# Two second norms folded into the stages of the first norms (latent attention and Mamba block)

## The chip, the cores and the metric

The kernel runs on one core of a Trainium2 chip. The metric is the device time of one execution in microseconds; the time before is the median of three runs.

## The reference, cut to what matters

Six blocks in a row, each of them added to its input and normalised. The second block begins with a layer norm of the first's already normalised output, the fourth with an RMS norm of the third's.

```python
x = _layernorm(x + _L0_attn_ref(x, ...), axis=-1)
x = _layernorm(x + _L0_xattn_ref(ctx_1024, x, ...), axis=-1)   # begins: ln = layernorm(latents=x, ln_l_g, ln_l_b)
x = _layernorm(x + _L0_ffn_ref(x, ...), axis=-1)
x = _layernorm(x + _L1_attn_ref(x, ...), axis=-1)              # begins: xn = x * rsqrt(mean(x**2) + 1e-6) * norm_scale
x = _layernorm(x + _L1_xattn_ref(x, ctx_1024, ...), axis=-1)
x = _layernorm(x + _L1_ffn_ref(x, ...), axis=-1)
```

x has 32 batches of 56 rows of 128 features, 1792 rows in all, float32. The layer norm has an epsilon of 1e-5. For a row with variance v the first norm's output has mean 0 and variance v / (v + 1e-5), so both norms in a row can be had from v alone: the layer norm of the layer norm divides by the root of (1 + 1e-5) v + 1e-10, the RMS norm of it by the root of (1 + 1e-6) v + 1e-11.

## The kernel before, in words

The rows are held as 16 tiles of 112 rows (`x_tm`), in 4 chunks of 4 tiles. The program is a sequence of blocks; in each, every engine has a written-out queue, and the queues meet by semaphores. Between blocks all engines wait for each other. After the larger stages (`lent_semaphores`, L107) two more barriers and a clearing of semaphores follow.

First place. `stage_scan` runs the first block's scan and leaves its gated result in `gT`, transposed. Then `stage_norm` "l0p" runs: TensorE adds x and the output projection in PSUM (L295, L766), VectorE takes the statistics of each row from there (bn_stats L312, bn_aggr L316), ScalarE the root (L354), VectorE the reciprocal and the normalised rows (L328, L334), written to `x_tm`. The loop on VectorE takes the statistics of chunk c and then normalises chunk c - 1. Barriers follow. `stage_latents` then calls `stage_norm` "bln", which takes statistics of `x_tm` again, writes normalised rows to `keep`, transposes them on TensorE (L301) and evicts them with gain and shift on ScalarE (L366) to `lT`. Beside it SP issues ten small loads and four context loads of 750 KB (L833 to L843), and POOL two memsets. The first eviction waits for the ten small loads. The block after it ("bw") opens with TensorE's products of `lT` (L890).

Second place. `stage_weighed` "f0r" is the tail of the third block (two of eight experts per row): TensorE projects each expert's hidden rows (L1656) into four PSUM banks, half a tile's experts to a bank; VectorE weighs and adds them into `z` (L1577), in a written-out interleaved order, takes statistics (L1592, L1596), reciprocal (L1602) and offset (L1604); ScalarE writes the normalised rows from `z` to `x_tm` (L1560). SP loads the Mamba block's weights beside it. Barriers follow. `stage_mamba` then calls `stage_norm` "min" (an RMS norm: two small products more per chunk, L321 and L323; eviction L364 with the gain to `xnT`), and its next block opens with TensorE's products of `xnT` (L1915).

Of the kernel before, what the change touches and what calls it, by code (L numbers as in the profile page):

```python
# [16 lines left out]
ALU = mybir.AluOpType  # L17
# [25 lines left out]
LN_EPS = 1e-5  # L43
DT_TOP = 0.11
# [127 lines left out]
class MambaWeights:  # L172
# [12 lines left out]
    bout: object  # L185
    loaded: object
# [6 lines left out]
def mamba_weights(core, ctx):  # L193

    H2 = INNER // P
    sb, _ = ctx.enter_context(scope(core, "mw"))
    core.mamba = MambaWeights(
        col=sb("col", [P, H2, 12]), alog=sb("alog", [P, H2, DS]), scale=sb("scale", [D, 1]), win=sb("win", [D, 2 * INNER]),
        wdt_in=sb("wdt_in", [P, H2, MAMBA_R]), wdt_out=sb("wdt_out", [MAMBA_R, INNER]), dtb=sb("dtb", [MAMBA_R, 1]),
        wbc=sb("wbc", [P, H2, P]), bcb=sb("bcb", [P, 1]), wout=sb("wout", [P, H2, D]), bout=sb("bout", [T2, D]),  # L200
        loaded=core.sem("mw_loaded"))
# [59 lines left out]
def stage_norm(core, name, project=None, doubled=False, rms=False, gain=None, shift=None,  # L261
               residual=True, outT=None, beside=None, ready=None):
# [7 lines left out]
    squared, roots = core.shared("n_squared"), core.shared("n_roots")  # L270
    with scope(core, name) as (sb, psum):
        y = psum("y", [P, NC, 512]) if project else None
        xt = psum("xt", [P, NC, 512]) if outT else None
        keep = core.x_tm if residual else sb("keep", [T2, NT, D])
        raw = sb("raw", [T2, NT, 6])
        mv = sb("mv", [T2, NT, 2])
        rstd = sb("rstd", [T2, NT])
        std = sb("std", [T2, NT])
# [7 lines left out]
        with nc.Block() as block:  # L286
# [19 lines left out]
            def _(ve):  # L306
# [18 lines left out]
                def normalise(c):  # L325
                    tiles = slice(c * TPC, (c + 1) * TPC)
                    ve.wait_ge(roots.sem, roots(c + 1))
                    ve.reciprocal(rstd[:, tiles], std[:, tiles]).then_inc(scales.sem, 1)  # L328
                    ve.wait_ge(scales.sem, scales(c + 1))
                    for n in range(c * TPC, (c + 1) * TPC):  # L330
                        if rms:
                            last = ve.tensor_scalar(keep[:, n, :], value(n), rstd[:, n:n + 1], None, ALU.mult)
                        else:
                            last = ve.tensor_scalar(keep[:, n, :], value(n), mv[:, n, 0:1], rstd[:, n:n + 1], ALU.subtract, ALU.mult)  # L334
                    last.then_inc(normed.sem, 1)

                for c in range(NC + 1):
# [6 lines left out]
            def _(act):  # L344
# [3 lines left out]
                for c in range(NC + 2):  # L348
                    if c < NC:
                        if rms:  # L350
                            act.wait_ge(squared.sem, squared(2 * c + 2))
                        else:
                            act.wait_ge(moments.sem, moments(c + 1))
                        act.activation(std[:, c * TPC:(c + 1) * TPC], mv[:, c * TPC:(c + 1) * TPC, 1], ACT.Sqrt,  # L354
                                       bias=eps[0:T2, :]).then_inc(roots.sem, 1)
                    if c >= 2 and outT:
# [24 lines left out]
        roots.base += NC  # L381
        normed.base += NC
# [24 lines left out]
def stage_scan(core):  # L407
# [4 lines left out]
    with scope(core, "l0s") as (sb, psum):  # L412
        gT = sb("gT", [P, 2, T])
        wout = sb("wout", [P, 2, D])

        with scope(core, "l0r") as (sb2, psum2):
            u = sb2("u", [P, RC, TC, 2, W])
            yT = sb2("yT", [P, 2, NCH, TC * B])
            gate = sb2("gate", [P, 2, NCH, TC * B])
            xs = sb2("xs", [P, 2, NCH, TC * B])  # L420
            xr = sb2("xr", [P, NCH, D])
            xnT = sb2("xnT", [D, NCH, TC * B])
            win = sb2("win", [D, 2 * INNER])
            lnw = sb2("lnw", [D, 2])
            raw = sb2("raw", [P, NCH, 6])
            mv = sb2("mv", [P, NCH, 2])
            rstd = sb2("rstd", [P, NCH])
            shift = sb2("shift", [P, NCH])
            eb = sb2("eb", [P, 2, RB // CPG, CPG, DS])
            cexp = sb2("cexp", [P, NG, RB])  # L430
            bcol = sb2("bcol", [P, 2, DS])
            spread = sb2("spread", [P, RB])
            c_gp = sb2("c_gp", [NG, 2, P])
            cA = sb2("cA", [P, 2, NG])
            mine = sb2("mine", [P, CPG])
            a_col = sb2("a_col", [P, 1])
            NPU = 6
            pu = psum2("pu", [P, NPU, 512])
            py = psum2("py", [P, 512])
            pg = psum2("pg", [P, 512])  # L440
            names = ("const built mine turned got spread eb cexp step u_made filled filled_ve y_made y_taken y_gated x_made x_kept "
                     "stats moments lnv rstd shift normed xturned xT").split()
            s = {n: core.sem(f"l0r_{n}") for n in names}
            x_first, x_rest, loads_x, loads_w, loads_p, loads_late = (core.sem(f"l0r_load_{n}") for n in
                                                                    ("first", "rest", "x", "w", "p", "late"))

            half_way = NCH // 2
            WAVES = 4
            FILLS = WAVES * 4
            SHARED = FILLS // 2  # L450

            def scanned(t):

                return 2 + 4 * t

            def wave(w):

                return w // 2, 2 * (w % 2)

            def filling(n):  # L460

                return (s["filled_ve"], n // 2 + 1) if n < FILLS and n % 2 else (s["filled"], n // 2 + 1 if n < FILLS else n - SHARED + 1)

            PAIRS = NCH // 2
            REST = slice(1, NCH - 1)
            def load_x(eng, tiles, sem):
                for k in range(TC):
                    src = d["x"].rearrange("b (j t) d -> t b j d", t=TC)[k]
                    eng.dma_start(xr[k * B:(k + 1) * B, tiles, :], src[:, tiles, :]).then_inc(sem, 16)

            kept = [("x", p) for p in range(RC + 1)]
            for c in range(PAIRS):
                if RC + 1 + c < PAIRS:
                    kept.append(("x", RC + 1 + c))
                kept.append(("gate", c))

            def kept_at(what, p):

                return kept.index((what, p)) + 1

            with nc.Block() as block:
                @block.sync
                def _(sp):
                    sp.dma_start(bcol[:, :, :], d["L0_attn_B_mat"].rearrange("(h p) s -> p h s", p=P)).then_inc(loads_p, 16)
                    load_x(sp, pair_of_chunks(0), x_first)
                    sp.dma_start(c_gp[:, 0, :], d["L0_attn_C_mat"].rearrange("(g i) s -> g (i s)", i=CPG)).then_inc(loads_x, 16)
                    sp.dma_start(c_gp[:, 1, :], d["L0_attn_A_log"].rearrange("(g i) s -> g (i s)", i=CPG)).then_inc(loads_x, 16)
                    sp.wait_ge(x_first, 16 * TC)
                    sp.dma_start(wout[:, :, :], d["L0_attn_out_proj_wT"].rearrange("(h p) d -> p h d", p=P)).then_inc(loads_late, 16)
                    sp.dma_start(core.x_tm[:, :, :], d["x"].rearrange("b t d -> (b t) d")  # L490
                                 .rearrange("(n p) d -> p n d", p=T2)).then_inc(loads_late, 16)
                    sp.wait_ge(loads_late, 32)

                @block.gpsimd
                def _(pool):
# [281 lines left out]
LP = 64  # L777

def stage_attention(core):  # L780

# [1914 lines left out]
```

## Time and profile before

| | us |
|---|---|
| median of three runs | 1248.31 (1247.03 to 1248.79) |
| profiled execution, its own time | 1245.21 |
| its span, first to last instruction | 1243.5 |
| VectorE ends the scan | 244.61 |
| first norm's rows written | 260.08 |
| block after the second norm opens on TensorE | 274.87 |
| expert stage's rows written | 793.45 |
| block after the RMS norm opens on TensorE | 807.04 |

Times in the profile count from the span's start. PE is TensorE's matmul queue and PEld its weight loads, DVE is VectorE, ACT ScalarE, POOL GpSimd, SP the queue that issues loads.
### The profile page before, as it was taken

To read this page: it belongs to the slowest core of one execution; us is meant where nothing else is said; L and a number is where in the kernel's file an instruction comes from. 1 tells how busy PE (TensorE), PEld (TensorE's weight loads), DVE (VectorE), ACT (ScalarE), POOL (GpSimd) and SP (SyncE) were. 2 spreads that over 40 slices of the span, in tenths; PEclk is the share of its full clock that TensorE was granted. 3 is DMA by queue.
4 is the path that set the end of the run, shared out by engine and by line. 5 is a ranking of instruction groups with operands and counts; after the bars stand their busy time and mean duration, and the time that the engine had idled before them with its cause. 6 is when DMAs were issued, how large, how long until landed. Compare 5 with 4: busy or idle time off the path is not lost. (4 is left out here: it accounts for less than half of the span.)

```text
span 1243.5 us, 22989 instructions
## 1 busy us (share of the span) xinstructions
PE 1020.0 (82%) x8317; PEld 742.0 (60%) x8317; DVE 1007.7 (81%) x2073; ACT 714.9 (57%) x1508; POOL 592.1 (48%) x899
## 2 busy tenths in 40 slices
PE   5889996557599999999999698391788888768696
PEld 3555653234599999999998566340333333536555
DVE  5989999665698889889886538778999999577575
ACT  3677673025466666666664263275677777247453
POOL 4200000002798888888884131011799999225360
PEclk9899998768799999999999989795799999879989
DMA  3000000011301211112100010001000000000001
GB/s 74 1 1 2 2 1 1 1 53 60 132 32 71 76 72 67 66 73 76 71 6 2 1 24 1 1 1 42 25 0 1 1 1 1 1 2 3 2 1 30
DMA packets 18770, 33.41 MB, mean 27 GB/s; under 512 B 5201, under 2 KB 13889, under 8 KB 18657
## 3 DMA queue, kind: packets, MB, share of 16 engines
q1 hardware_dynamic: 16768, 30.89, 7.3%
q10 hardware_dynamic: 1888, 1.05, 0.4%
q8 instruction: 66, 1.08, 0.4%
q14 instruction: 48, 0.39, 0.1%
HBM read 31.02 MB, written 0.92 MB: 26 GB/s over the span
## 5 line engine op out<-in xcount | busy, mean ns | idle before, releaser
L2209 POOL TENSOR_TENSOR m_h_in<-m_dtu,m_bs 128x448 f32<-128x448 f32 x128 | 144.3, 1146 | 70.3 <-DVE m_dtu L2253 53.4
L753 DVE SCALAR_TENSOR_TENSOR l0r_u<-l0r_u,l0r_a_col 128x1024 f32<-128x1024 f32 x110 | 135.9, 1276 | 6.0 <-ACT l0r_u L663 6.0
L2276 DVE TENSOR_TENSOR_SCAN m_hs<-msp_da,m_h_in 128x448 f32<-128x448 f32 x128 | 136.0, 1078 | 2.4 <-ACT msp_da L2236 1.7
L1134 POOL TENSOR_TENSOR bl_sc<-bl_sc,bl_topall 125x1456 f32<-125x1456 f32 x32 | 105.3, 3289 | 59.6 <-ACT bl_topall L1296 59.6
L663 ACT ACTIVATE l0r_u<-l0r_pu 128x512 f32<-128x512 f32 x216 | 108.4, 644 | 32.3 <-PE l0r_pu L565 32.2
L2172 PE MATMUL msp_py<-m_hc,ident 128*128 128x448 f32 x256 | 118.1, 546 | 0.0
L565 PE MATMUL l0r_pu<-l0r_xs,l0r_eb 32*128 32x256 f32 x896 | 106.5, 460 | 6.9 <-ACT l0r_u L663 4.6
L846 POOL MEMSET bq_lT<- 128x256 f32 x1 | 0.3, 311 | 222.1 <-POOLq L107 222.1
L1371 PE MATMUL bl_pS<-b_qw,bl_xcT 128*125 128x112 f32 x768 | 104.0, 278 | 0.0
L565 PEld LDWEIGHTS l0r_pu<-l0r_xs,l0r_eb 32*128 32x128 f32 x896 | 73.0, 210 | 39.5 <-ACT l0r_u L663 29.0
L2227 ACT ACTIVATE m_bs<-msp_pb 128x448 f32<-128x448 f32 x128 | 69.2, 541 | 44.9 <-PE msp_pb L2156 43.4
L1303 ACT ACTIVATE bl_sq<-bl_pX 125x512 f32<-125x512 f32 x96 | 57.2, 597 | 63.2 <-PE bl_pX L1360 34.5
L1371 PEld LDWEIGHTS bl_pS<-b_qw,bl_xcT 128*125 128x125 f32 x768 | 91.5, 189 | 0.0
L1360 PE MATMUL bl_pX<-b_mk,bl_xcT 128*125 128x128 f32 x768 | 91.4, 277 | 0.0
L1360 PEld LDWEIGHTS bl_pX<-b_mk,bl_xcT 128*125 128x125 f32 x768 | 88.2, 191 | 0.2 <-ACT bl_xcT L1241 0.2
L1211 DVE TENSOR_REDUCE bl_top<-bl_sc 125x112 f32<-125x1456 f32 x32 | 86.3, 2696 | 1.5 <-DVE bl_sc L1191 0.5
L2236 ACT ACTIVATE msp_da<-m_dt,mw_alog 128x440 f32<-128x440 f32 x128 | 80.2, 627 | 5.5 <-DVE m_hs L2276 5.5
L1191 DVE TENSOR_TENSOR bl_sc<-bl_pS,bl_inv 125x448 f32<-125x448 f32 x96 | 59.1, 620 | 26.9 <-PE bl_pS L1371 26.9
L1225 DVE TENSOR_REDUCE bl_ss<-bl_sq 125x8 f32<-125x512 f32 x96 | 62.7, 680 | 14.3 <-ACT bl_sq L1303 10.4
L2164 PE MATMUL msp_pc<-m_bc,selector 128*128 128x448 bf16 x128 | 47.6, 372 | 31.9 <-DVE m_hc L2262 31.9
L2164 PEld LDWEIGHTS msp_pc<-m_bc,selector 128*128 128x128 bf16 x128 | 12.5, 98 | 102.6 <-DVE m_hc L2262 94.6
L758 DVE TENSOR_SCALAR l0r_u<-l0r_u 128x1024 f32<-128x1024 f32 x112 | 72.0, 683 | 0.0
(396 smaller groups left out, 2527.6 us busy)
## 6 DMA issues: line engine op xcount, KB each, us to landing
b_xc<-in_ctx SPq DMA_DIRECT2D x16, 750.0 KB
bl_more<-in_ctx SPq DMA_DIRECT2D x16, 750.0 KB
x_tm<-in_x SPq DMA_DIRECT2D x1, 896.0 KB, 6.2
cw_cT<-in_ctx_headT SPq DMA_DIRECT2D x1, 896.0 KB
out_dram<-x_tm SPq DMA_DIRECT2D x4, 224.0 KB, 2.5
l0r_xr<-in_x ACTq DMA_DIRECT2D x4, 192.0 KB, 5.5
w_up<-in_L_ffn_w SPq DMA_DIRECT2D x1, 512.0 KB, 4.0
w_down<-in_L_ffn_w SPq DMA_DIRECT2D x1, 512.0 KB, 5.2
```

The costliest lines, as they stand in the source:

```text
L565: last = pe.matmul(out, eb[rows, half, j0 + j, :, :], x, start=True, stop=True)
L663: act.activation(u[:, c % RC, :, :, at:at + 2 * B].rearrange("p t r x -> p (t r) x"), pu[:, n % NPU, :].rearrange("p (a x) -> p a x", x=2 ...
L753: ve.scalar_tensor_tensor(state(c, i, r), prev, a_col[:, :], state(c, i, r), ALU.mult, ALU.add).then_inc(s["step"], 1)
L758: ve.tensor_scalar(state(c, i, r), state(c, i, r), 10.0, -10.0, ALU.min, ALU.max).then_inc(s["step"], 1)
L1134: pool.tensor_tensor(sc[0:KP, n % 3, :, :], sc[0:KP, n % 3, :, :], over(topall[0:KP, n % 2, :].unsqueeze(1), [KP, KT + 1, QR]), ALU.subtra ...
L1211: ve.tensor_reduce(top[0:KP, n % 2, :], sc[0:KP, n % 3, :, :].rearrange("p k q -> p q k"), AX, ALU.max).then_inc(s["top"], 1)
L1360: last = pe.matmul(pX[0:KP, u, r * D:(r + 1) * D], xcT[:, n % 2, at], mk[:, :], start=True, stop=True)
L1371: last = pe.matmul(pS[0:KP, u, r * QR:(r + 1) * QR], xcT[:, n % 2, t * KP:(t + 1) * KP], qw[:, n, :], start=False, stop=(r == KS - 1))
L2172: pe.matmul(py[:, g % 2, 0:CH], core.ident[:, :], hc[:, n % NU, :], start=(st == 0), stop=(st == DS - 1)).then_inc(s["summed"], 1)
L2209: pool.tensor_tensor(h_in[:, n % NU, :], dtu[:, half, cols], bs[:, n % NU, :], ALU.mult).then_inc(s["db"], 1)
L2236: act.activation(da[:, n % 2, 0:CH].rearrange("p (b t) -> p b t", t=L)[:, :, 1:L], dt[:, half, cols].rearrange("p (b t) -> p b t", t=L)[:, ...
L2276: ve.tensor_tensor_scan(hs[:, n % NU, :], da[:, n % 2, 0:CH], h_in[:, n % NU, :], 0.0, ALU.mult, ALU.add).then_inc(s["scan"], 1)
```

## The change

First place: "l0p" and "bln" become one call of `stage_norm`, made by `stage_latents` after the scan's barriers. It takes the row statistics once, computes two roots per chunk, writes the second norm's rows with VectorE to `keep`, and the first norm's rows with ScalarE from PSUM to `x_tm`, in ScalarE's queue ahead of the evictions. ScalarE reads a PSUM bank only after VectorE has done with it. SP's loads and POOL's memsets of "bln" now run beside it. `gT` is now two tensors, the first of them `core.xT`, which is free then; the expert weights' buffers are laid out ahead of the scan.

Second place: the "min" call is gone. In the expert stage VectorE computes both reciprocals and writes the RMS norm's rows to `keep` after each chunk's scale; TensorE transposes them behind its last projection into the banks (`ph`) that the hidden products used; ScalarE evicts them with the gain to `mamba.xnT`.

```diff
 def stage_norm(core, name, project=None, doubled=False, rms=False, gain=None, shift=None,
-               residual=True, outT=None, beside=None, ready=None):
+               residual=True, outT=None, beside=None, ready=None, second=False):
...
-        keep = core.x_tm if residual else sb("keep", [T2, NT, D])
+        keep = core.x_tm if residual and not second else sb("keep", [T2, NT, D])
+        R2 = 2 if second else 1
...
-                    ve.reciprocal(rstd[:, tiles], std[:, tiles]).then_inc(scales.sem, 1)
+                    ve.reciprocal(rstd[:, :, tiles], std[:, :, tiles]).then_inc(scales.sem, 1)
                     ve.wait_ge(scales.sem, scales(c + 1))
+                    if second:
+                        ve.scalar_tensor_tensor(offset[:, tiles], mv[:, tiles, 0], -1.0, rstd[:, 0, tiles], ALU.mult,
+                                                ALU.mult).then_inc(offsets.sem, 1)
...
+                        if second:
+                            if c == 0:
+                                act.wait_ge(offsets.sem, offsets(1))
+                            act.activation(std[:, 1, c * TPC:(c + 1) * TPC], mv[:, c * TPC:(c + 1) * TPC, 1], ACT.Sqrt,
+                                           bias=next_eps[:, :], scale=1.0 + LN_EPS)
...
+                    if second and 1 <= c < NC + 1:
+                        act.wait_ge(offsets.sem, offsets(c + 1))
+                        act.wait_ge(normed.sem, normed(c))
+                        for n in range((c - 1) * TPC, c * TPC):
+                            act.activation(core.x_tm[:, n, :], value(n), ACT.Identity, bias=offset[:, n:n + 1],
+                                           scale=rstd[:, 0, n:n + 1])
                     if c >= 2 and outT:
...
-        stage_norm(core, "l0p", project=project)
+    return project
...
-        stage_norm(core, "bln", residual=False, gain=lng[:, 2:3], shift=lng[:, 3:4],
+        stage_norm(core, "l0p", project=gated_projection, second=True, gain=lng[:, 2:3], shift=lng[:, 3:4],
...
+                opened(pe)
+                for c in range(NC):
+                    pe.wait_ge(s["rows"], c + 1)
+                    for r in range(TPC):
+                        last = pe.transpose(ph[:, c, r * T2:(r + 1) * T2], keep[:, c * TPC + r, :], core.ident[0:T2, 0:T2])
+                    last.then_inc(s["turned"], 1)
...
-                for c in range(NC + 1):
+                act.wait_ge(s["next_eps"], 1)
+                act.wait_ge(core.mamba.loaded, MAMBA_LOADED)
+                for c in range(NC + 2):
                     if c < NC:
                         tiles = slice(c * TPC, (c + 1) * TPC)
                         act.wait_ge(s["moments"], c + 1)
-                        act.activation(std[:, tiles], mv[:, tiles, 1], ACT.Sqrt, bias=core.eps_ln[0:T2, :]).then_inc(s["roots"], 1)
-                    if c:
+                        act.activation(std[:, 0, tiles], mv[:, tiles, 1], ACT.Sqrt, bias=core.eps_ln[0:T2, :])
+                        act.activation(std[:, 1, tiles], mv[:, tiles, 1], ACT.Sqrt, bias=next_eps[:, :],
+                                       scale=1.0 + RMS_EPS).then_inc(s["roots"], 1)
+                    if 1 <= c < NC + 1:
                         act.wait_ge(s["scales"], 2 * c)
...
+                    if c >= 2:
+                        act.wait_ge(s["turned"], c - 1)
+                        act.activation(inputs[:, (c - 2) * CH:(c - 1) * CH], ph[:, c - 2, 0:CH], ACT.Copy, scale=core.mamba.scale[:, 0:1])
...
+                def next_rows(c):
+
+                    ve.wait_ge(s["scales"], 2 * c + 1)
+                    for n in range(c * TPC, (c + 1) * TPC):
+                        last = ve.tensor_scalar(keep[:, n, :], z[:, n, :], mv[:, n, 0:1], rstd[:, 1, n:n + 1], ALU.subtract, ALU.mult)
+                    last.then_inc(s["rows"], 1)
+
                 for c in range(NC + 1):
                     if c < NC:
                         statistics(c)
                     if c:
                         scale_and_offset(c - 1)
+                        next_rows(c - 1)
...
-            stage_norm(core, "min", rms=True, residual=False, gain=scale[:, 0:1], outT=by_batch(xnT),
-                       ready=(core.mamba.loaded, MAMBA_LOADED))
...
-        with lent_semaphores(core):
-            stage_scan(core)
         expert_weights(core)
-        with lent_semaphores(core):
-            stage_attention(core)
+        with ExitStack() as gated_scope:
+            with lent_semaphores(core):
+                gated_projection = stage_scan(core, gated_scope)
+            with lent_semaphores(core):
+                stage_attention(core, gated_projection)
```

## Rows read from the trace of the kernel before

**Rows 1.** The page, busy time by engine
```profile
PE 1020.0 (82%) x8317; PEld 742.0 (60%) x8317; DVE 1007.7 (81%) x2073; ACT 714.9 (57%) x1508; POOL 592.1 (48%) x899
```

**Rows 2.** Timeline around the first place: start us, us, engine, line
```profile
243.51 1.10 DVE L718 TENSOR_TENSOR l0s_gT<-l0r_py,l0r_gate 128x256 f32<-128x256 f32 x2 [7.20 <-PE l0r_py L585]
...
244.94 0.44 PE L295 MATMUL l0p_y<-x_tm,ident 112*112 112x128 f32 x2 [1.50 <-PEq L481]
...
253.15 0.88 DVE L312 BATCH_NORM_STATS2 l0p_raw<-l0p_y 112x6 f32<-112x128 f32 x4
...
255.10 0.60 PE L766 MATMUL l0p_y<-l0s_wout,l0s_gT 128*112 128x128 f32 x4
255.83 0.88 DVE L312 BATCH_NORM_STATS2 l0p_raw<-l0p_y 112x6 f32<-112x128 f32 x4
...
258.71 1.37 DVE L334 TENSOR_SCALAR x_tm<-l0p_y,l0p_mv,l0p_rstd 112x128 f32<-112x128 f32 x4
...
261.75 0.87 DVE L312 BATCH_NORM_STATS2 bln_raw<-x_tm 112x6 f32<-112x128 f32 x4 [1.68 <-PEq L107]
...
264.30 1.11 DVE L334 TENSOR_SCALAR bln_keep<-x_tm,bln_mv,bln_rstd 112x128 f32<-112x128 f32 x4
...
265.47 1.01 PE L301 MATMUL bln_xt<-ident,bln_keep 112*128 112x112 f32 x4 [9.77 <-DVE bln_keep L334]
...
270.47 0.72 ACT L366 ACTIVATE bq_lT<-bln_xt,bq_lng 128x448 f32<-128x448 f32 x1 [3.53 <-DMA bq_mask<-in_mask_BxS_bk]
...
271.28 1.33 ACT L366 ACTIVATE bq_lT<-bln_xt,bq_lng 128x448 f32<-128x448 f32 x2
...
274.87 4.77 PE L890 MATMUL bw_ps<-bq_w,bq_lT 128*128 128x384 f32 x8 [1.06 <-PEq L286]
...
287.35 0.91 PE L890 MATMUL bw_ps<-bq_w,bq_lT 128*128 128x384 f32 x2 [2.33 <-ACT b_vl L962]
```

**Rows 3.** Timeline around the second place
```profile
770.60 0.15 DVE L1602 RECIPROCAL f0r_rstd<-f0r_std 112x4 f32<-112x4 f32 x1
...
770.86 0.34 DVE L1577 SCALAR_TENSOR_TENSOR f0r_z<-f0r_pj,f0r_used,x_tm 112x128 f32<-112x128 f32 x1
...
783.04 3.19 PE L1656 MATMUL f0r_pj<-w_down,f_hidden 128*112 128x128 f32 x24 [1.65 <-DVE f0r_z L1577]
...
789.89 0.14 DVE L1602 RECIPROCAL f0r_rstd<-f0r_std 112x4 f32<-112x4 f32 x1
...
790.27 3.18 ACT L1560 ACTIVATE x_tm<-f0r_z,f0r_offset,f0r_rstd 112x128 f32<-112x128 f32 x8
...
794.58 0.87 DVE L312 BATCH_NORM_STATS2 min_raw<-x_tm 112x6 f32<-112x128 f32 x4 [3.86 <-PEq L107]
...
806.11 0.63 ACT L364 ACTIVATE mi_xnT<-min_xt,mw_scale 128x448 f32<-128x448 f32 x1 [0.37 <-PE min_xt L301]
...
807.04 8.36 PE L1915 MATMUL mip_ps<-mi_xnT,mw_win 128*128 128x448 f32 x16 [0.97 <-PEq L286]
```

**Rows 4.** Windows: PE, PEld, DVE, ACT, POOL busy; PEclk, DMA share, GB/s
```profile
244.90:255.70 10.80, 10.76 (x96) 10.59 (x96) 6.36 (x34) 2.38 (x5) 0.00 (x0) 1.00 0.00 1
255.70:261.00 5.30, 0.00 (x1) 0.00 (x0) 4.27 (x19) 0.30 (x1) 0.00 (x0) 0.75 0.00 0
274.87:278.87 4.00, 4.00 (x7) 2.19 (x8) 0.74 (x8) 1.10 (x4) 0.00 (x0) 0.51 0.33 137
289.00:290.00 1.00, 1.00 (x7) 1.00 (x6) 0.00 (x0) 0.12 (x2) 1.00 (x1) 0.53 0.32 135
770.00:786.00 16.00, 12.32 (x101) 11.11 (x100) 15.77 (x70) 3.82 (x10) 0.00 (x0) 1.00 0.01 2
786.00:794.00 8.00, 0.23 (x3) 0.03 (x1) 4.37 (x21) 3.44 (x9) 0.00 (x0) 0.80 0.00 0
```

**Rows 5.** One line of ScalarE: an affine copy from PSUM, min/median/max ns
```profile
L639 ACT ACTIVATE l0r_xnT<-l0r_pg,l0r_lnw x7: 558/564/637, 10.2 to 92.1; 128x256 f32<-128x256 f32 x7
```

**Rows 6.** Timeline of SP's queue in the expert stage
```profile
725.83 0.47 SPq L223 DMA_DIRECT2D mw_bcb<-in_L_attn_c_proj_b  x1
```

More of the change, by code:

```diff
@@ L43 @@
 LN_EPS = 1e-5
+RMS_EPS = 1e-6
 DT_TOP = 0.11
@@ L185 @@
     bout: object
+    xnT: object
     loaded: object
@@ L269, in stage_norm @@
         core.shared(s) for s in ("n_proj", "n_stats", "n_moments", "n_scales", "n_normed", "n_turned"))
-    squared, roots = core.shared("n_squared"), core.shared("n_roots")
+    squared, roots, offsets = (core.shared(s) for s in ("n_squared", "n_roots", "n_offsets"))
     with scope(core, name) as (sb, psum):
@@ L381, in stage_norm @@
         roots.base += NC
+        offsets.base += NC + 1 if second else 0
         normed.base += NC
@@ L764, in project @@
-        def project(pe, n, out):
-            for h in range(2):
-                last = pe.matmul(out, gT[:, h, n * T2:(n + 1) * T2], wout[:, h, :], start=False, stop=(h == 1))
-            return last
-        stage_norm(core, "l0p", project=project)
+                                if j == 0 and n >= NPU:
+                                    pe.wait_ge(*filling(n - NPU))
+                                rows = slice(gl * RB, (gl + 1) * RB)
+                                out = pu[:, n % NPU, :].rearrange("p (t r j b) -> p j r t b", t=TC, r=2, j=2)[:, j]
@@ new lines, in _ @@
+                pe.wait_ge(s["built"], 1)
+                turn(0)
+                pe.wait_ge(loads_w, 32)
+                project("x", 0)
+                pe.wait_ge(loads_x, 32)
+                for k in range(2):
+                    pe.transpose(pu[:, NPU - 1, k * NG:(k + 1) * NG], c_gp[:, k, :], core.ident[0:NG, 0:NG]).then_inc(s["turned"], 1)
+                pe.wait_ge(s["eb"], 1)
+                pe.wait_ge(s["got"], 2)
+                for c in range(RC):
+                    inputs(c)
+                    turn(c + 1)
+                    project("x", c + 1)
@@ L772, with project @@
+    def project(pe, n, out):
+        for h in range(2):
+            last = pe.matmul(out, gT[h][:, n * T2:(n + 1) * T2], wout[:, h, :], start=False, stop=(h == 1))
+        return last
+    return project
 HB, DH = 2, 64
@@ L777, with stage_attention @@
 LP = 64
[L780 removed]
+def stage_attention(core, gated_projection):
     nc, d = core.nc, core.dram
@@ L1474, in route, with stage_weighed @@
     chain.base += 5
-def stage_weighed(core, name, products, openings, mixes, project, expert):
+def stage_weighed(core, name, ph, products, openings, opened, mixes, project, expert):
     nc = core.nc
```

666 lines of the change are left out of this document (329 added, 337 removed).

## The prediction

> **What bounds the kernel now.** I read the page first for the shape of the whole, then the lines of instructions in order of time at the two places that the diff touches, then the windows that give TensorE's granted clock there. The page [rows 1] shows TensorE and VectorE busy over 80% of the span and DMA far from full, but this says little about the change: the program is a row of stages with a block end between each two, and what an edit is worth is read inside its own stage. Both edited places are serial strips in which no engine is full.
>
> First place [rows 2]: VectorE ends the scan at 243.51 + 1.10 = 244.61, and TensorE opens the output projection at 244.94. VectorE ends that first norm at 258.71 + 1.37 = 260.08, and the separate second norm begins at 261.75, behind two barriers. TensorE opens the following stage at 274.87. The strip from 244.61 to 274.87 is 30.26 us.
>
> Second place [rows 3]: the last moments of the expert stage are ready when VectorE issues its next reciprocal at 789.89; ScalarE ends the rows at 790.27 + 3.18 = 793.45; the RMS norm opens at 794.58, its last eviction ends at 806.11 + 0.63 = 806.74, and TensorE opens the Mamba stage at 807.04.
>
> **First place, part by part.** Removed: a whole pass of 16 bn_stats, 16 bn_aggr, 4 square roots, 4 reciprocals and the chain of four chunks that waited on each other (261.75 to 274.87), with a 3.53 us wait of ScalarE for the last of the stage's own loads [rows 2]. Moved: the barrier now stands before the projection instead of after it; the ten small loads and the four context loads on SP's queue, and POOL's two memsets, go with it to the start of the merged stage. Added: a second square root per chunk, one VectorE offset per chunk, and 16 ScalarE activations that write the residual rows from PSUM.
>
> The barrier. The handover with barrier took VectorE 261.75 - 260.08 = 1.67 us, the one without took TensorE 244.94 - 244.61 = 0.33 [rows 2]. The merged stage's first matmul is at 244.61 + 1.67 = about 246.3, 1.35 later than before. It isn't a loss: the same barrier is gone from further on.
>
> VectorE's queue. Its chunks began 2.68 us apart (253.15 and 255.83) [rows 2]. The offset costs what it costs in the expert stage: from the reciprocal to the next weighing 0.26 us (770.60 to 770.86), of which the reciprocal is 0.15 [rows 3], so 0.1 a chunk; the reciprocal is twice as wide, still 8 columns, nothing. The rows themselves are still one pass from PSUM.
>
> TensorE's queue. It now holds, between the projections of chunks 2 and 3, a wait for chunk 0's normalised rows and four transposes. Projections of chunk 2 end at 255.70 - 2.65 + 1.35 = 254.4 (255.10 + 0.60 = 255.70 is the end of the last [rows 2], 2.65 a quarter of 10.76 us of matmul [rows 4]); chunk 0's rows are ready at 254.6. The transposes took 1.01 us at the lower clock [rows 2]; at the upper I take 0.75. Chunk 3's projections then run 255.4 to 258.05, and VectorE's last statistics start at 258.15 instead of 255.83. From there VectorE needed 260.08 - 255.83 = 4.25 us; with two offsets 4.45, so 262.6.
>
> ScalarE's queue sets the end. Eight row activations took 3.18 us from SBUF [rows 3]; from PSUM with the same operands there is no row, and I take the same. Bounds: the 256-column one from PSUM with both operands takes 0.564 [rows 5], which would make eight cost at most 1.3 us more, and nothing in a row suggests less. [...] Chunk 2's rows can start when VectorE has used that bank, one chunk (1.37 for its rows, some 0.25 for reciprocal and offset) before its own end, at 261.0. Behind them in ScalarE's queue are the eviction of chunk 1, chunk 3's rows, and the evictions of chunks 2 and 3: 3.18 + 3 x 0.67 (1.33 for two [rows 2]) = 5.2. ScalarE ends at 266.2, and the next stage opens 0.3 later (806.74 to 807.04 at the other place [rows 3]), at 266.5. Gain: 8.4 us. The loads: the last released ScalarE 8.7 us after the second norm's start (261.75 to 270.47) [rows 2]; from 246.3 that is 255.0, and ScalarE asks at about 259, so the wait is covered by 4 us. The context loads start 15 us earlier; nobody waits for them at either time.
>
> The clock. TensorE now stops from 243.44 (end of the scan's sums, 1.50 before 244.94) to 246.3, for 2.9 us. The projections ran at the upper level, 2.4 GHz, granted 1.00 [rows 4]. What stops did to it: after 255.70 the grant averaged 0.75 over 5.3 us, so it fell 2.65 us into the stop; after 786.23 it fell 4.6 us in (0.80 over 8 us from 786); after a stop of 2.33 us before 287.35 it fell at about 289.1, when TensorE was running again (0.53); stops of 1.65 us in the expert stage changed nothing [rows 2 to 4]. So 2.9 us is on the side where a fall came. Price: a fully fed TensorE stayed low for the 4.0 us from 274.87 (0.51) [rows 4], and loses half, 2 us. Since chunk 3's projections set VectorE's last chunk, it comes straight off: 6.4 us. I take the fall, gain 6.4; bounds 6.4 and 8.4. The Trainium skill ("TensorE: Matmul & The Clock Gate", Part 1: The HAM clock gate) says that the gate runs free of the program, so that the same kernel meets it at different points. By that rule either value can come from the same code; the trace agrees only in that stops of similar length ended differently.
>
> **Second place, part by part.** Removed: the RMS norm's block, 794.58 to 806.74, with 16 bn_stats, 16 bn_aggr, 8 small products, its square roots, and its chain. Added on VectorE: four rows per chunk from SBUF, 1.11 us for four (264.30) plus a gap, 1.15 [rows 2]; four chunks. VectorE is the full engine in the expert stage (15.77 of 16 us [rows 4]), so the two chunks' worth ahead of the last statistics, 2.3 us, push the last moments from 789.89 to 792.2. Then two reciprocals with offsets (0.26 each) and two chunks of rows: 795.0. Added on TensorE: transposes. Those of chunks 0 and 1 stand behind the last product (783.04 + 3.19 = 786.23, now 788.5) and are done by 790.5; nobody needs them sooner. ScalarE blocks on the first of them from about 783 to 789.3, with nothing queued behind it that VectorE needs before 792.2. Then ScalarE, which sets the end again: two square roots 792.3 to 792.85, rows of chunk 2 1.6, eviction of chunk 1 0.62, rows of chunk 3 1.6, evictions 0.62 twice (0.63 the last one [rows 3]): 5.06 in sum, 797.9. Its wait for the Mamba weights is free: SP had issued the last of those loads by 726.3 [rows 6], 30 us before ScalarE would ask. The handover with barrier (793.45 to 794.58, TensorE a little later) 1.3: the Mamba stage opens at 799.2. Gain 7.8 us. Bounds: evictions and rows could overlap better (0.5 more) or VectorE's rows cost 1.37 as from PSUM (1.0 less in all).
>
> TensorE's stops at chunk ends in the expert stage grow from 1.65 [rows 3] to 2.8 us, and the clock may fall in there. I cost it at nothing: TensorE is up to four half tiles ahead of VectorE (four banks), each about 1.08 us of VectorE, and a low stretch of 4 us puts it back by 2 us. Without that lead each of the two would cost up to 2 us.
>
> **The sum.** 6.4 + 7.8 = 14.2 us off the profiled execution: span 1243.5 to 1229.3, its time 1245.2 to 1231.0. The median of the runs stands 3.1 above that execution: 1248.3 - 14.2 = 1234.1; I say 1234.
>
> **Rivals.** (a) No fall of the clock at the first projection: 1232. For it: a stop ended by a running TensorE, and the scan's sums ran at full grant just before. Against: the 2.33 us case. (b) The gaps at the ends have become so short that the next stages also open at the upper clock (before, they did not, after 19 and 21 us with little matmul): 2 us each more, 1228 to 1230. Against: TensorE has still only a few transposes in the last 8 us of either place. (c) The ScalarE tails are longer than I think, because activations from PSUM cost the higher bound and each turn between engines some 0.1 us, and the lead doesn't cover a fall in the expert stage: 1.3 + 1 + 2 = 4.3 less gain, 1238. (d) Slower than before: the stages behind are moved against the clock gate, and the context stage behind them meets the lower level more often. A fully fed stretch of 4 us low costs 2; it decides only from 8 further such stretches in its path (16.7 us), and against it stands that the stage keeps TensorE fed, whereas all the falls that I read follow a stop. 1251 or more. (e) The change doesn't shorten the first place, because the first eviction waits for the loads: they would have to land over 4 us later than from the same queue before, and each further microsecond costs one; all gain of that place gone, 1240.
>
> **How the numbers follow.** Forecast 0.46, its own range 1232.8 to 1235.8. (a) 0.22, (b) 0.08, (c) 0.16, (d) 0.05, (e) 0.03. Eight in ten: from (b)'s upper part to (c)'s end with the spread of a median of three (1247.0 to 1248.8): 1229.5 to 1238.5. Within 0.2% of before (2.5 us, about what a measurement of this kernel can tell from no change) lies the lesser part of (d), 0.02, above it the rest, 0.03; faster 0.95.
>
> **What would show each step.** First matmul of the merged stage about 1.7 us behind the scan's end; VectorE's last statistics start 11.9 us (14 with a fall) behind that matmul; granted clock there; no DMA wait in front of the first eviction; ScalarE last in the stage, about 3.6 us behind VectorE's last rows; eight row activations in some 3.2 us. At the second place the last moments 2.3 us later than before against the stage's start, ScalarE last again, and the Mamba stage opening 7.0 us behind those moments. Wrong would make it: a row activation of 0.56 us, a new wait of ScalarE for transposes after the last moments, or a clock that stays low through the expert stage.

## The result

The changed kernel takes 1236.86 us (median of four runs, 1235.67 to 1238.35) against 1248.55 before: a ratio of 0.9886 [0.985, 0.9923]. Run again beside other kernels (e8) it was at 1237.12, ratio 0.9918 [0.99, 0.9936]; that is 9.9 us under the 1247.04 of before beside it, where 11 to 13 had been expected. The forecast was 1234.0, range 1229.5 to 1238.5, faster. The median gain is 11.7 us where 14.2 were forecast; between the two profiled executions it is 9.6.

The table gives the lengths of the parts, each from the first start of one instruction to the first start of another, in one profiled execution of each kernel. "Strip" is from the scan's last gated product to the latents' products; "latents" from there to the context stage's first bn_stats; "moments" from the first to the last bn_aggr of the expert stage (the operation that leaves a tile's mean and variance), "tail" from there to the Mamba stage's first product.

| kernel | scan ends | strip | latents | moments | tail | span |
|---|---|---|---|---|---|---|
| before | 244.0 | 30.9 | 38.1 | 29.2 | 17.2 | 1243.5 |
| changed | 244.8 | 22.1 | 39.2 | 35.7 | 6.6 | 1233.9 |
| changed, again | 246.3 | 22.1 | 39.2 | 35.8 | 6.6 | 1235.4 |
| e1, first place only | 256.6 | 23.8 | 38.1 | 29.2 | 17.4 | 1255.0 |
| e2, second place only | 244.0 | 31.0 | 38.0 | 33.8 | 6.4 | 1242.6 |
| e3, rows spread | 247.7 | 22.1 | 39.1 | 30.8 | 6.6 | 1234.6 |
| e4, TensorE fed | 247.7 | 23.8 | 38.0 | 31.3 | 6.6 | 1236.0 |
| e5, before with padding | 243.3 | 31.2 | 37.8 | 33.7 | 17.2 | 1251.9 |
| e6, rows on POOL | 242.4 | 23.8 | 38.0 | 29.3 | 6.6 | 1228.9 |
| e7, tuned | 247.9 | 20.0 | 38.2 | 29.4 | 5.2 | 1226.4 |
| e9, ends kept warm | 245.1 | 19.7 | 36.1 | 29.5 | 4.7 | 1220.2 |

The first place gained 8.8 us in the strip (6.4 forecast) and gave back 1.1 in the latents' stage. The second gained 4.1 us (46.4 to 42.3) where 7.8 were forecast. The rest of the profiled difference of 9.6 us is in parts that the change doesn't touch: the scan ended 0.8 later, and from the second block's norm to the expert stage's routing took 18.2 us instead of 16.7 (the granted clock was 0.50 over the first 3.15 us of that norm's projections, 1.00 before the change); the others balance. The profiled execution of e10 was a disturbed one, so only its times are told.

### The profile page after: what moved, and what is told of

It reads as the page before. It is cut to its first block and busy times, and to the rows that moved or that the text cites. A ratio compares the mean times of both kernels' runs of the same rounds, so it can differ in the third digit from the quotient of the medians.

```text
span 1233.9 us, 22903 instructions
## 1 busy us (share of the span) xinstructions
PE 1025.5 (83%) x8317; PEld 747.9 (61%) x8317; DVE 993.4 (81%) x1983; ACT 719.5 (58%) x1522; POOL 594.7 (48%) x899
## 5 line engine op out<-in xcount | busy, mean ns | idle before, releaser
L1324 ACT ACTIVATE bl_sq<-bl_pX 125x512 f32<-125x512 f32 x96 | 57.2, 597 | 61.3 <-PE bl_pX L1381 33.0
```

## The profile after

The first place in the timeline of the changed kernel (start us, us, engine, line); it answers to [rows 2]:

```profile
244.83 0.63 DVE L739 TENSOR_TENSOR l0s_gT<-l0r_py,l0r_gate 128x256 f32<-128x256 f32 x1
...
247.22 0.44 PE L300 MATMUL l0p_y<-x_tm,ident 112*112 112x128 f32 x2 [2.94 <-PEq L108]
...
258.95 0.89 DVE L317 BATCH_NORM_STATS2 l0p_raw<-l0p_y 112x6 f32<-112x128 f32 x4 [0.56 <-PE l0p_y L787]
...
261.92 1.50 ACT L375 ACTIVATE x_tm<-l0p_y,l0p_offset,l0p_rstd 112x128 f32<-112x128 f32 x4 [0.93 <-DVE l0p_keep L342]
...
262.04 1.36 DVE L342 TENSOR_SCALAR l0p_keep<-l0p_y,l0p_mv,l0p_rstd 112x128 f32<-112x128 f32 x4
263.30 0.73 ACT L387 ACTIVATE bq_lT<-l0p_xt,bq_lng 128x448 f32<-128x448 f32 x1
...
263.91 1.52 ACT L375 ACTIVATE x_tm<-l0p_y,l0p_offset,l0p_rstd 112x128 f32<-112x128 f32 x4
265.28 1.38 ACT L387 ACTIVATE bq_lT<-l0p_xt,bq_lng 128x448 f32<-128x448 f32 x2
...
266.96 5.46 PE L911 MATMUL bw_ps<-bq_w,bq_lT 128*128 128x384 f32 x8 [2.49 <-PEq L291]
```

TensorE opens 247.22 - 245.46 = 1.76 us behind the scan (1.7 forecast) after a stop of 2.94. The last statistics start 11.73 behind that (11.9 forecast without a fall of the clock); they wait 0.56 us for chunk 3's projections, which stand behind the transposes (0.60 at the upper clock, 0.75 taken). VectorE ends at 263.40, ScalarE at 266.66, 3.3 later (3.6 forecast), with exactly the queue of the forecast: rows, eviction, rows, two evictions. Four row activations from PSUM take 1.50 to 1.52 us, less than half of the 3.18 that [rows 3] gave for eight from SBUF, and less than the 1.63 to 1.64 of four from SBUF in this same trace; the upper bound of the prediction, 0.564 each, is out. The Trainium skill, "ScalarE: Activation LUTs", section What ACT_TABLE_LOAD costs, has a formula in which the source memory doesn't appear; the estimate by it is 1.64 for four, 8% high here and right for SBUF. No eviction waits for a load.

The second place of the same kernel; it answers to [rows 3]:

```profile
765.17 1.11 DVE L1648 TENSOR_SCALAR f0r_keep<-f0r_z,f0r_mv,f0r_rstd 112x128 f32<-112x128 f32 x4
...
768.27 0.34 DVE L1614 SCALAR_TENSOR_TENSOR f0r_z<-f0r_pj,f0r_used,x_tm 112x128 f32<-112x128 f32 x1
...
768.41 8.49 PE L1701 MATMUL f0r_pj<-w_down,f_hidden 128*112 128x128 f32 x48 [2.70 <-DVE f0r_z L1614]
...
772.20 0.35 DVE L1614 SCALAR_TENSOR_TENSOR f0r_z<-f0r_pj,f0r_used,x_tm 112x128 f32<-112x128 f32 x1 [1.78 <-PE f0r_pj L1701]
...
775.19 0.35 DVE L1614 SCALAR_TENSOR_TENSOR f0r_z<-f0r_pj,f0r_used,x_tm 112x128 f32<-112x128 f32 x1 [0.83 <-PE f0r_pj L1701]
...
782.11 5.46 PE L1701 MATMUL f0r_pj<-w_down,f_hidden 128*112 128x128 f32 x24 [2.70 <-DVE f0r_z L1614]
...
790.71 0.17 DVE L1639 RECIPROCAL f0r_rstd<-f0r_std 112x8 f32<-112x8 f32 x1
...
793.28 1.64 ACT L1594 ACTIVATE x_tm<-f0r_z,f0r_offset,f0r_rstd 112x128 f32<-112x128 f32 x4
...
794.82 1.14 ACT L1598 ACTIVATE mw_xnT<-f_ph,mw_scale 128x448 f32<-128x448 f32 x2
...
797.24 8.56 PE L1962 MATMUL mip_ps<-mw_xnT,mw_win 128*128 128x448 f32 x16 [2.73 <-PEq L108]
```

Here the forecast fails, between the first and the last moments: behind the rows of chunk 0 (765.17) and of chunk 1 TensorE stops for 2.70 us instead of 1.65, and the 48 matmuls after it take 8.49 us, where 32 take 4.07 at the upper clock. VectorE, busy for 15.77 of 16 us here before [rows 4], waits 1.78 + 0.83 us for TensorE behind the first stop and 1.78 (at 785.90) behind the second, 4.4 in all. After the last statistics all is as forecast: the Mamba stage opens 6.5 us behind the reciprocal at 790.71 (7.0), ScalarE last: from 792.76 to its end at 795.96 it never waits.

The granted clock in the same places (PE, PEld, DVE, ACT, POOL busy; PEclk, DMA share, GB/s); it answers to [rows 4]:

```profile
247.20:258.75 11.55, 11.20 (x100) 11.02 (x101) 6.84 (x37) 4.58 (x13) 1.58 (x2) 1.00 0.26 68
...
766.00:769.00 3.00, 0.59 (x3) 0.59 (x4) 3.00 (x13) 1.03 (x3) 0.00 (x0) 0.79 0.00 0
769.00:773.00 4.00, 4.00 (x20) 4.00 (x20) 2.22 (x10) 0.00 (x0) 0.00 (x0) 0.50 0.01 4
773.00:779.00 6.00, 5.49 (x43) 5.29 (x42) 5.06 (x25) 0.29 (x2) 0.00 (x0) 0.87 0.00 0
...
782.00:786.00 4.00, 3.89 (x18) 3.90 (x19) 2.22 (x10) 0.00 (x0) 0.00 (x0) 0.50 0.00 0
...
266.96:272.42 5.46, 5.46 (x9) 3.04 (x10) 0.74 (x8) 1.66 (x6) 0.00 (x0) 0.50 0.33 132
```

The projections ran at 1.00 after their 2.94 us stop. The products behind the two 2.70 us stops of the expert stage opened at 0.50. A mean of 0.79 is 0.42 of the time at 0.50 and the rest at 1.00, so the three windows from 766 to 779 hold 3.00 x 0.42 + 4.00 + 6.00 x 0.26 = 6.8 us at 0.50 (the grant fell about 2 us into the stop and rose about 6.2 us after TensorE had restarted); the second low stretch, 781.41 to 788.24, is as long.

## The experiments

**e1 and e2: one place each.** e1 is the changed kernel with the expert stage and the "min" call of before; e2 is the kernel before with both of the changed kernel's.

```diff
 # e1: changed kernel
-                        next_rows(c - 1)
...
+            stage_norm(core, "min", rms=True, residual=False, gain=scale[:, 0:1], outT=by_batch(xnT),
+                       ready=(core.mamba.loaded, MAMBA_LOADED))
```

> Only the first place merged; the expert stage and the RMS norm as before. If the gains of the two places add, the strip from the scan's end to the latents' products is 21.5 us as in the changed kernel (30.3 before), and the time is 6 to 8.5 us under before. The rival, that the latents' stage gives back what it won (its first products at the lower clock for longer, 2.2 us lost between that point and the expert stage in the one profile of the changed kernel), gives 6 at the most; if the 2.2 is only where the clock gate happened to fall, 8 to 9.

> Only the second place merged. Clock theory: TensorE's two stops at chunk ends in the expert stage are 2.7 us instead of 1.65, the granted clock falls behind them, VectorE waits 1.8 us or more for TensorE after each, and the place gains 4 us instead of the 7.8 forecast. The rival, that the falls in the one profile were chance, gives 7 to 8 us here.

e1: 1244.51 us, ratio 0.9958 [0.9936, 0.9979]. e2: 1245.55, ratio 0.9981 [0.9952, 1.001], not told from no change. The two ratios make 0.994 together and not the 0.989 of both, so they don't settle the division; their intervals reach 2.7 and 3.6 us to either side. Each ratio holds one execution far from its others: 1256.68 in e1 (the profiled one; the next is 1246.02), 1259.18 in e2 (the next is 1248.78). By the medians of the same executions e1 is 5.9 and e2 5.4 us under before, 11.3 together. The parts divide it: e1's strip and latents together are 61.9 us, the changed kernel's 61.3, the kernel before's 69.0, so the first place is worth 7 to 8 us. e2's moments and tail are 40.2 us against 46.4: 6.2, where 4 were expected and its rival had 7 to 8. The stops are 2.70 us as expected, but VectorE's waits behind them are 1.40 and 1.16 us, not 1.8 or more, where the changed kernel has 4.4 in all:

```profile
781.12 0.35 DVE L1595 SCALAR_TENSOR_TENSOR f0r_z<-f0r_pj,f0r_used,x_tm 112x128 f32<-112x128 f32 x1 [1.40 <-PE f0r_pj L1682]
...
793.27 0.35 DVE L1595 SCALAR_TENSOR_TENSOR f0r_z<-f0r_pj,f0r_used,x_tm 112x128 f32<-112x128 f32 x1 [1.16 <-PE f0r_pj L1682]
```

In e2 the grant was 0.50 from 777.14 to 780.56 and from 790.80 to 794.21, 3.4 us each, half of the 6.8 in the changed kernel. What set the length of a low stretch was not found.

e1's trace shows the fall that the prediction put into the projections. Its timeline and windows:

```profile
258.94 0.44 PE L299 MATMUL l0p_y<-x_tm,ident 112*112 112x128 f32 x2 [2.94 <-PEq L108]
...
259.88 0.38 PE L786 MATMUL l0p_y<-l0s_wout,xT 128*112 128x128 f32 x2
...
260.35 0.63 PE L299 MATMUL l0p_y<-x_tm,ident 112*112 112x128 f32 x2
```

```profile
258.90:262.00 3.10, 3.06 (x20) 3.09 (x21) 0.06 (x1) 1.49 (x2) 1.60 (x2) 0.72 0.26 67
262.00:266.00 4.00, 4.00 (x31) 4.00 (x30) 1.27 (x8) 0.49 (x2) 0.00 (x0) 0.79 0.30 39
```

A pair of matmuls takes 0.63 us from 260.35 on, where it took 0.38 before, for some 3 us (0.50 from 260.28 to 263.69). The strip is 23.8 us instead of 22.1. The stop in front was 2.94 us here as in the changed kernel's profile, where nothing fell: behind the same stop either came about. Of the eight executions in the table with the merged first place, three (e1, e4, e6) have it.

**e3 and e4: the same work without the long stop.** In e3 the next norm's rows of chunks 0 and 1 are issued one tile at a time:

```diff
 # weigh_chunk(c), changed kernel
                             if n:
                                 weigh(n - 1, 1, r)
+                        if c >= 2:
+                            next_row((c - 2) * TPC + n - c * TPC - 1)
...
-                        next_rows(c - 1)
+                        if c >= NC - 1:
+                            next_rows(c - 1)
```

> Changed kernel, but the next norm's rows of chunks 0 and 1 are issued one tile (0.28 us) at a time between the weighings of a later chunk, so VectorE does the same work and TensorE's stop at a chunk end is 1.6 us again. Clock theory: no fall, no wait of VectorE for TensorE after the first chunk, 4.4 us faster than the changed kernel, some 16 under before. Rival (the work on VectorE and the order of the queues cost it, not the clock): as the changed kernel, 11 to 12 under before.

In e4 VectorE's queue is left alone and TensorE gets work that nobody reads:

```diff
 # TensorE's queue in the expert stage, changed kernel
+                        if m in (21, 29):
+                            opened(pe)
+                            for _ in range(10):
+                                pe.matmul(ph[:, NC - 1, 0:P], core.ident[:, :], core.ident[:, :], start=True, stop=True)
                         if m >= 4:
                             pe.wait_ge(s["weighed"], ...)
```

> Changed kernel with ten matmuls on the identity (2.1 us at the upper clock, results unused) in TensorE's queue in each of the two stops; VectorE's queue is untouched. Clock theory: the clock stays at 1.00, VectorE's 4.4 us of waits are gone, 4 us faster than the changed kernel. Rival (queue order, VectorE's work): no gain, or slower because TensorE has more to do.

Timelines, first of e3, then of e4:

```profile
769.90 0.34 DVE L1619 TENSOR_SCALAR f0r_keep<-f0r_z,f0r_mv,f0r_rstd 112x128 f32<-112x128 f32 x1
...
770.04 2.00 PE L1710 MATMUL f0r_pj<-w_down,f_hidden 128*112 128x128 f32 x16 [1.68 <-DVE f0r_z L1614]
...
772.37 2.00 PE L1710 MATMUL f0r_pj<-w_down,f_hidden 128*112 128x128 f32 x16 [0.33 <-DVE f0r_z L1614]
```

```profile
770.79 2.40 PE L1569 MATMUL f_ph<-ident 128*128 128x128 f32 x20
773.65 4.07 PE L1705 MATMUL f0r_pj<-w_down,f_hidden 128*112 128x128 f32 x32 [0.47 <-DVE f0r_z L1618]
```

In e3 the stop behind chunk 0 is 1.68 us (1.80 behind chunk 1), the ones after it 0.33. In e4 the added matmuls fill each stop but for 0.47 us, and the 32 products behind them take 4.07. In both the grant is 1.00 from 768 to 786 and VectorE doesn't wait for TensorE. Moments falls from 35.7 to 30.8 and 31.3 us, the 4.4 us of waits (and 0.5 more in e3); in e4 this happens although TensorE has more to do than in the changed kernel, which refutes both rivals (VectorE's work, the order of the queues). Whole: e3 1237.18, ratio 0.9895 [0.9855, 0.9936], 13.5 us under the 1250.71 of before where some 16 were expected; e4 1234.16, ratio 0.9875 [0.9851, 0.9898]. Against the changed kernel's two ratios (0.9886 and 0.9918) their intervals overlap; the 4.4 us are read from the part, not from the whole.

**e5: the stop alone, in the kernel before.** Nothing of the change, but VectorE's four row operations behind the first two offsets, into a tile that nobody reads:

```diff
 # kernel before, VectorE in the expert stage
                     if c:
                         scale_and_offset(c - 1)
+                    if c in (1, 2):
+                        for n in range((c - 1) * TPC, c * TPC):
+                            ve.tensor_scalar(pad[:, n, :], z[:, n, :], mv[:, n, 0:1], rstd[:, n:n + 1], ALU.subtract, ALU.mult)
```

> The kernel before, with four row operations of VectorE (1.15 us, into a spare tile, results unused) behind each of the first two offsets of the expert stage: the place and length that the changed kernel's rows have there, and nothing else of the change. Clock theory: TensorE's stops go from 1.65 to 2.7 us, the grant falls after one or both, and the span from first to last moments grows by 2.3 us of work plus 2 to 4.4 us of waiting for TensorE (29.2 to 33.5 or 35.7). Rival (the waiting comes from the new transposes or the new order): 29.2 to 31.5.

1255.01 us, ratio 1.0055 [1.0035, 1.0076]. Timeline and windows:

```profile
776.74 5.10 PE L1660 MATMUL f0r_pj<-w_down,f_hidden 128*112 128x128 f32 x32 [2.67 <-DVE f0r_z L1578]
...
780.13 0.35 DVE L1578 SCALAR_TENSOR_TENSOR f0r_z<-f0r_pj,f0r_used,x_tm 112x128 f32<-112x128 f32 x1 [1.38 <-PE f0r_pj L1660]
...
789.09 4.54 PE L1660 MATMUL f0r_pj<-w_down,f_hidden 128*112 128x128 f32 x24 [2.67 <-DVE f0r_z L1578]
...
792.25 0.35 DVE L1578 SCALAR_TENSOR_TENSOR f0r_z<-f0r_pj,f0r_used,x_tm 112x128 f32<-112x128 f32 x1 [1.15 <-PE f0r_pj L1660]
```

```profile
776.00:780.00 4.00, 3.26 (x17) 3.26 (x18) 2.76 (x11) 0.00 (x0) 0.00 (x0) 0.57 0.02 4
...
789.00:793.00 4.00, 3.91 (x21) 3.91 (x22) 2.85 (x12) 0.00 (x0) 0.00 (x0) 0.60 0.00 0
```

The stops are 2.67 us where they were 1.65, and VectorE waits 1.38 and 1.15 us behind them. Moments is 33.7 us, 4.5 more: 2.5 of waits and 2.0 of work (33.5 was the lower figure of the clock theory; the rival said 31.5 at most). Here the grant was 0.50 for 3.4 us around or just behind the end of each stop (776.13 to 779.55, 789.79 to 793.20), as in e2, and not for 6.8 as in the changed kernel, so the waits are 2.5 in place of 4.4. e5 shows that the longer stop alone brings the fall; it doesn't show why the low stretch was twice as long in the changed kernel.

**e6: the rows of chunks 0 and 1 on POOL.**

```diff
 # POOL's queue in the expert stage, behind the odd squares
+                for c in range(NC - 2):
+                    pool.wait_ge(s["scales"], 2 * c + 1)
+                    for n in range(c * TPC, (c + 1) * TPC):
+                        last = pool.tensor_scalar(keep[:, n, :], z[:, n, :], mv[:, n, 0:1], rstd[:, 1, n:n + 1], ALU.subtract, ALU.mult)
+                    last.then_inc(s["pool_rows"], 1)
```

> Changed kernel, rows of chunks 0 and 1 computed by POOL, which idles there, instead of VectorE. Clock theory: stops of 1.7 us, no fall, first to last moments 29.3 us against 35.7 in the changed kernel: 6.4 us less. If POOL's reads slow VectorE beside it, up to 1 us of that is lost. Rival: as the changed kernel less 2.3.

1232.90 us, ratio 0.9885 [0.9866, 0.9905]; moments 29.3 us. Timeline:

```profile
765.55 3.15 POOL L1554 TENSOR_SCALAR f0r_keep<-f0r_z,f0r_mv,f0r_rstd 112x128 f32<-112x128 f32 x4 [12.67 <-DVE f0r_rstd L1647]
...
767.77 4.07 PE L1710 MATMUL f0r_pj<-w_down,f_hidden 128*112 128x128 f32 x32 [1.68 <-DVE f0r_z L1622]
```

POOL takes 3.15 us for what takes VectorE 1.11, in a time in which it has nothing else to do; TensorE's stop is 1.68, and VectorE's work beside it isn't slowed. In the runs made beside it the changed kernel had 1237.12 us and 0.9918 [0.99, 0.9936], 4.2 us more than this one: the right side, with intervals that just overlap. The 6.4 us expected stand in the part alone.

**e7 and e10: a tuned kernel.** Rows of chunks 0 to 2 on POOL; reciprocal and offset after the first tile of the next chunk, so that only chunk 3 is left behind the last statistics; at the first place the transposes of chunk 0 behind chunk 3's projections, the residual rows of chunk 3 on VectorE, the eviction of chunk 1 before the rows of chunk 2.

```diff
 # first place, VectorE
                     last.then_inc(normed.sem, 1)
+                    if second and c == NC - 1:
+                        for n in range(c * TPC, (c + 1) * TPC):
+                            ve.tensor_scalar(core.x_tm[:, n, :], value(n), mv[:, n, 0:1], rstd[:, 0, n:n + 1], ALU.subtract, ALU.mult)
...
 # expert stage, weigh_chunk(c)
+                        if c and n == c * TPC + 1:
+                            scale_and_offset(c - 1)
```

> Candidate. Expert stage: rows of chunks 0 to 2 on POOL, reciprocals and offsets issued after the first tile of the next chunk, so that only chunk 3 is behind the last statistics. First place: the transposes of chunk 0 behind the projections of chunk 3, the residual rows of chunk 3 on VectorE, eviction of chunk 1 before the rows of chunk 2. If the tail on ScalarE sets the end of both stages: first place 2 us shorter than the changed kernel's 19.8, second place from last moments to the Mamba stage 5.1 instead of 6.6 us and 29.3 between first and last moments; together 10 us under the changed kernel, 21 under before. If VectorE's rows or TensorE set the ends instead, the first place gains 0.5 at the most.

> The tuned candidate once more, beside the one above: 18 to 21 us under before, 17.6 us (19.2 with a fall of the clock in the projections) from first projection to the latents' products, 29.4 and 5.2 us in the expert stage's last two parts.

e7: 1230.33 us, ratio 0.9847 [0.9824, 0.9871]; e10: 1229.75, ratio 0.9834 [0.9807, 0.9861]. e7's parts are as expected: from first projection to the latents' products 17.6 us (19.7 in the changed kernel), moments 29.4, tail 5.2. The whole falls short: 6.8 us under the changed kernel and 16.7 under before by the medians, where 10 and 21 were expected. e10 is 19.7 under before, inside its 18 to 21. The last statistics of the first place start 11.09 us behind the first projection (250.29 to 261.38) instead of 11.73, so TensorE's order gives 0.6 of the 2.1 us and the shorter tail the other 1.5. e7's timelines, first place and then the expert stage's tail:

```profile
250.29 0.44 PE L300 MATMUL l0p_y<-x_tm,ident 112*112 112x128 f32 x2 [2.94 <-PEq L108]
...
261.38 0.88 DVE L319 BATCH_NORM_STATS2 l0p_raw<-l0p_y 112x6 f32<-112x128 f32 x4
```

```profile
784.26 0.16 DVE L1667 SCALAR_TENSOR_TENSOR f0r_offset<-f0r_mv,f0r_rstd 112x4 f32<-112x4 f32 x1
784.34 1.11 DVE L1674 TENSOR_SCALAR f0r_keep<-f0r_z,f0r_mv,f0r_rstd 112x128 f32<-112x128 f32 x4
784.46 1.65 ACT L1620 ACTIVATE x_tm<-f0r_z,f0r_offset,f0r_rstd 112x128 f32<-112x128 f32 x4
...
785.50 1.01 PE L1592 MATMUL f_ph<-ident,f0r_keep 112*128 112x112 f32 x4 [4.51 <-DVE f0r_keep L1674]
786.55 0.63 ACT L1605 ACTIVATE mw_xnT<-f_ph,mw_scale 128x448 f32<-128x448 f32 x1 [0.44 <-PE f_ph L1592]
...
788.47 7.66 PE L1986 MATMUL mip_ps<-mw_xnT,mw_win 128*128 128x448 f32 x16 [1.96 <-PEq L108]
```

Behind the offset stand only one chunk's rows, its transposes and its eviction; ScalarE writes the residual rows meanwhile, and its last eviction now waits 0.44 us for the transposes. At the first place, where ScalarE's queue was shortened and VectorE's rows for the transposes were not, this shows that ScalarE's tail did set the end. At the second place e7 takes chunk 2's rows and offset off VectorE's tail too, so its 1.4 us don't tell the two tails apart; there the trace of the changed kernel speaks, in which ScalarE runs to its end without a wait and starts its last two evictions 0.3 us after the last transposes ended.

**e9: TensorE kept fed to the ends.** The tuned kernel with matmuls on the identity in TensorE's pauses, results unused:

```diff
 # first place, behind the transposes of chunks 1 and 2
+                        if second and 1 <= t < NC - 1:
+                            for _ in range((9, 4)[t - 1]):
+                                pe.matmul(xt[:, NC - 1, 0:P], core.ident[:, :], core.ident[:, :], start=True, stop=True)
 # expert stage, behind the transposes of chunks 2 and 3
+                    if c >= NC - 2:
+                        for _ in range((20, 2)[c - NC + 2]):
+                            pe.matmul(ph[:, NC - 1, 0:P] if c < NC - 1 else pj[:, 0, 0:P], core.ident[:, :], core.ident[:, :],
+                                      start=True, stop=True)
```

> The tuned candidate with matmuls on the identity (results unused) in TensorE's pauses at the ends of both places: nine and four before the last two transposes of the first place, twenty before and two after the last transposes of the second. This tries rival (b) of the prediction. If a TensorE that never pauses for more than about 2 us keeps its clock, the latents' products open at 1.00 and the part from them to the context stage shrinks by 1.5 to 2 us (38.2 to 36.5), and the Mamba stage's first products open at 1.00, 1.5 to 2 us there: 3 to 4 us under the tuned candidate. If the clock falls all the same in the handovers, nothing, or up to 1 us slower at the transposes behind the added matmuls.

1224.11 us, ratio 0.9802 [0.9777, 0.9828]. Timeline and windows:

```profile
264.79 2.82 PE L925 MATMUL bw_ps<-bq_w,bq_lT 128*128 128x384 f32 x8 [1.11 <-PEq L291]
```

```profile
782.85 0.60 PE L1595 MATMUL f_ph<-ident,f0r_keep 112*128 112x112 f32 x4
...
785.40 6.25 PE L1993 MATMUL mip_ps<-mw_xnT,mw_win 128*128 128x448 f32 x16 [1.50 <-PEq L108]
```

```profile
260.00:266.00 6.00, 4.67 (x33) 3.71 (x32) 5.00 (x23) 4.79 (x13) 0.00 (x0) 1.00 0.32 131
266.00:272.00 6.00, 6.00 (x21) 3.78 (x21) 1.71 (x3) 4.50 (x17) 2.18 (x2) 1.00 0.32 133
...
788.00:792.00 4.00, 4.00 (x12) 2.03 (x11) 4.00 (x4) 3.43 (x6) 2.55 (x1) 1.00 0.00 0
```

The eight latents' products take 2.82 us instead of 5.46 in the changed kernel and 5.07 in e7, the Mamba stage's sixteen 6.25 instead of 8.56 and 7.66 ([rows 2] and [rows 3] had 4.77 and 8.36), the grant is 1.00 in all three windows, and the handovers of 1.1 and 1.5 us didn't lower it. The latents' stage shrinks by 2.1 us (38.2 to 36.1), the transposes of the last chunk from 1.01 to 0.60. This is the fastest version, 25 us under before by the medians (1249.45), and 5.6 under e10 where 3 to 4 were expected; the two intervals of the ratios overlap by 0.002.

## Why the prediction came out as it did

- **Barrier, offset, VectorE's and TensorE's queue at the first place: right**, each within 0.2 us.
- **ScalarE's tail sets the end of both stages: right.** At the first place e7 shows it, in which the shorter tail moved the end by 1.5 us; at the second it is read from the changed kernel's trace (e7's 1.4 us there came with a shorter tail on VectorE as well).
- **The clock falls in the projections, 2 us: half right.** It fell in three of eight executions, at a price of 1.7 us (strip 23.8 against 22.1), and not in the changed kernel's two profiles. Rival (a) was what the profile had; the place then gained 8.8 us (8.4 worked out).
- **The latents' stage and the Mamba stage open as before: wrong by a little.** When the projections were at 1.00, the latents' products stayed low for 5.46 us instead of 4.0, and the stage took 39.2 instead of 38.1 us. e1, e4 and e6, with the fall, had 38.0 to 38.1. So some of what one fall costs the other gives back.
- **Second place: this step failed: "I cost it at nothing: TensorE is up to four half tiles ahead of VectorE (four banks)".** The fall itself was foreseen. The lead wasn't there: VectorE's written-out order interleaves the second half of one tile with the first of the next, so banks come free in pairs. TensorE restarts only when VectorE has used a pair (768.27) and is then two half tiles ahead, 2.2 us of VectorE's time; at the lower clock the next pair takes TensorE 3.8 us (768.41 to 772.20). The difference is the 1.78 us that the timeline shows, and 0.83 for the next pair. Two falls cost 4.4 us, where the prediction's own bound without a lead was "up to 2 us" each: it took a low stretch of 4 us, and these lasted 6.8. e3, e4 and e6 take the stop or its idleness away in three ways and the waits go with it each time; e5 makes it alone and has 2.5.
- **The sum.** 8.8 - 1.1 + 4.1 = 11.8 us from the two places, near the 11.7 of the medians; the forecast had 6.4 + 7.8 = 14.2. Two errors of opposite sign, 2.4 too little at the first place and 3.7 too much at the second, and 1.1 left out. That they partly cancel is luck, and so is part of the median's nearness: before stood 3.1 us above its profiled execution, the changed kernel 1.2 (1236.86 against 1235.67), and that execution was forecast at 1231.0.
- **Rival (c)** came nearest: 1236.86 lies outside the forecast's own range (1232.8 to 1235.8) and toward (c)'s 1238. Of its three parts only the last came true, that the lead doesn't cover a fall, and it cost 4.4 us where (c) had 2; ScalarE's activations and turns were not longer than assumed.
- **Rival (b)** (the next stages open at the upper clock) did not occur by itself, but its mechanism and its price hold: e9 makes it happen, and gains about 2 us at each end over e7. **Rivals (d) and (e)** were not seen. That the context stage varies (386.6 to 389.8 us between executions, in kernels with and without the change) was not taken apart.

Open: what made the low stretches of the expert stage 6.8 us in the changed kernel and 3.4 in e2 and e5; whether the scan's different ends (242.4 to 256.6 us, in code that all kernels share) are the clock alone.

## What to carry to other kernels

Before putting work into a full engine's queue, look at who stands still meanwhile: 1.15 us more on VectorE lengthened TensorE's stop from 1.65 to 2.70, and the clock made 2.2 us of waiting out of it each time. Count the lead of a producer at the moment it restarts, by the order in which its buffers come free, not by how many there are. Where an engine idles beside, give it the rows at a third of the speed; and where TensorE only waits for the end of a stage, matmuls that nobody reads can be worth more than their time.

## What the runs showed of the hardware

A stop of TensorE of 2.94 us in front of the same 10.5 us of matmuls was followed by a fall of the granted clock in three executions and by none in five; the Trainium skill ("TensorE: Matmul & The Clock Gate", Part 1: The HAM clock gate) says that the gate runs free of the program, and these executions agree. Stops of 2.67 and 2.70 us at chunk ends of the expert stage came with a fall of the grant each time, eight times in four executions (the changed kernel, e8, e2, e5), the fall between 0.7 us before TensorE's restart and 0.7 after it; stops of 1.65 to 1.80 us there never did. The starts of neighbouring affine activations of 112x128 stood 0.34 to 0.36 us apart when they read PSUM, 0.38 to 0.40 when they read SBUF.
